# First stage of a four-layer graph network: casting transfers from GpSimd, three bf16 adjacency buffers, x a graph ahead

## What is computed

```python
h = jnp.maximum(_layernorm(x, axis=-1), 0.0)
w = _masked_row_softmax(transpose(adj))    # rows: 1/degree where there is an edge
region = jnp.matmul(w, features)           # features = h
region = jnp.matmul(region, kernel_1) + bias_1
region = _batch_norm(region, gamma_1, beta_1)        # over all graphs and nodes
people = jnp.matmul(jnp.transpose(w, (0, 2, 1)), region)
people = jnp.matmul(people, kernel_2) + bias_2
people = _batch_norm(people, gamma_2, beta_2)
x = x + people
```

## Time and profile before

| | us |
|---|---|
| Median of 3 runs | 1920.06 |
| Lowest, highest | 1919.37, 1922.35 |
| Profiled execution | 1929.35 |
| Its span, first to last instruction | 1927.6 |
| TensorE busy | 1584.4 (82%) |
| VectorE busy | 1387.6 (72%) |
| ScalarE busy | 1212.3 (63%) |
| GpSimd busy | 124.2 (6%) |

### The profile page before, as it was taken

One profiled execution on the slowest core, in us unless ns is written; L12 is line 12 of the kernel. 1 busy time (PEld: TensorE's weight loads), 2 busy tenths in 40 slices (PEclk: granted clock), 3 DMA queues, 4 the chain that ended last, 5 costly groups with the idle time before them and its releaser, 6 DMA issues. The chain is left out here.

```text
span 1927.6 us, 34910 instructions
## 1 busy us (share of the span) xinstructions
PE 1584.4 (82%) x13252; PEld 1288.4 (67%) x13252; DVE 1387.6 (72%) x3809; ACT 1212.3 (63%) x1905; POOL 124.2 (6%) x73
## 2 busy tenths in 40 slices
PE   3878878699646879889898888988889988898873
PEld 3778778455344757768677686776868767686572
DVE  5666665488546668878888788887788877887663
ACT  4777777122136567777777677776677767776552
POOL 0100100000000000000000000000000000010000
PEclk9998989799857989999999999999999999999986
DMA  6777775267331102022030220302203022020111
GB/s 217 283 253 283 263 251 201 86 242 246 140 105 35 54 23 88 17 84 78 23 99 21 79 77 23 98 15 86 77 23 92 17 90 78 23 66 10 46 33 35
DMA packets 106156, 195.64 MB, mean 101 GB/s; under 512 B 9088, under 2 KB 58880, under 8 KB 103936
## 3 DMA queue, kind: packets, MB, share of 16 engines
q1 hardware_dynamic: 103680, 184.98, 29.4%
q10 hardware_dynamic: 2304, 8.39, 1.1%
HBM read 151.40 MB, written 41.94 MB: 100 GB/s over the span
## 5 line engine op out<-in xcount | busy, mean ns | idle before, releaser
L1278 PE MATMUL ps<-fac_A,mask_A 128*128 128x258 f16 x2048 | 236.9, 275 | 36.1 <-DVE prod L910 24.8
L1278 PE MATMUL ps<-fac_C,mask_C 128*128 128x258 f16 x2048 | 237.3, 275 | 18.1 <-DVE mask_C L928 12.7
L1278 PEld LDWEIGHTS ps<-fac_A,mask_A 128*128 128x128 fp8e4 x2048 | 199.0, 98 | 74.2 <-DVE prod L910 31.7
L1345 PE MATMUL ps<-hV,wts 128*128 128x129 f32 x2048 | 243.0, 276 | 3.5 <-DVE prod L910 1.8
L1345 PEld LDWEIGHTS ps<-hV,wts 128*128 128x128 f32 x2048 | 236.7, 193 | 4.7 <-DVE prod L910 2.3
L1278 PEld LDWEIGHTS ps<-fac_C,mask_C 128*128 128x128 fp8e4 x2048 | 198.2, 98 | 53.7 <-issue 7.6
L953 DVE SCALAR_TENSOR_TENSOR wts<-lk,wts 128x1024 f32<-128x1024 f32 x128 | 154.9, 1221 | 90.6 <-ACT wts L1199 90.6
L1198 ACT ACTIVATE lk<-ps 128x1024 f32<-128x1024 f32 x128 | 131.9, 1031 | 111.3 <-PE ps L1336 87.8
L299 ACT ACTIVATE maskT<-ps 128x1024 fp8e4<-128x1024 bf16 x128 | 130.3, 1018 | 75.9 <-PE ps L338 69.6
L1199 ACT ACTIVATE wts<-ps,shiftB 128x1024 f32<-128x1024 f32 x128 | 143.5, 1121 | 0.0
L1177 ACT ACTIVATE mask_C<-s_row,steep_t_C 128x1024 fp8e4<-128x1024 f32 x128 | 141.7, 1141 | 0.0
(11 more groups left out here) (248 smaller groups left out, 3372.0 us busy)
## 6 DMA issues: line engine op xcount, KB each, us to landing
adj_r<-in_adj SPq DMA_DIRECT2D x128, 512.0 KB, 5.8
maskT_scratch<-maskT SPq DMA_DIRECT2D x16, 1024.0 KB, 6.8
ring_A<-maskT_scratch SPq DMA_DIRECT2D x64, 256.0 KB, 3.2
off<-maskT_scratch SPq DMA_DIRECT2D x32, 512.0 KB, 6.5
ring_C<-maskT_scratch SPq DMA_DIRECT2D x64, 256.0 KB, 4.1
xa<-in_x SPq DMA_DIRECT2D x16, 512.0 KB, 4.1
whT_scratch<-whT_s ACTq DMA_DIRECT2D x16, 512.0 KB, 6.4
whT_b<-whT_scratch SPq DMA_DIRECT2D x16, 512.0 KB, 4.8
```

Of the source, the lines that this page charges most:

```text
L1278: last = nc.tensor.matmul(Q_SLOTS[c % 2][:, k, 0:XW], m_fp8[x][:, k, j, c * P:c * P + P], fac[x][:, k, j, :], start=(j == 0), stop=(j == T ...
L1345: last = nc.tensor.matmul(Q_SLOTS[c // 2 % 2][:, c % 2, 0:PW], wts[:, j, c * P:c * P + P], hV[b % 2][:, j, :], start=(j == 0), stop=(j == ...
```

## The change

All of it is in the first stage and the set-up block ahead of it. `g_acc`, the raw row buffers `adj_r` and VectorE's casts are gone.

- GpSimd issues transfers that read int32 rows from HBM and write bf16 into `adj_b`, which now has three graph buffers. `load_adj(pool, b)` issues eight of 512 KB read. Graph 0 is issued in the set-up block, graph 1 ahead of the first power, graph 2 behind it, and graph b + 2 behind the power for graph b. From graph 3 on the issue waits until all products of the graph that used the buffer are done.
- x has two buffers. SP loads the first two in the set-up block and graph b after `a_h` of graph b - 2.
- VectorE normalises (`normed`, eight instructions), then clips while it writes the high part (`high`) and clips and subtracts for the low part (`low`). ScalarE's `normed` is gone. VectorE waits for the power in `shifts` at c = 3.
- The Gram product accumulates in its PSUM bank over all graphs, and the moments block reads the bank.
- whT is kept in two halves of 256 KB, one at c = 7 of the same graph, one at c = 3 of the next. TensorE waits for a kept half at the first and fifth `sums`.
- TensorE begins a graph's transposes when the eight transfers have landed, and waits for `a_h` only ahead of the first product.
- Memsets in the first stage shrink to the columns that need ones.

```diff
-            adj_r = sba("adj_r", [P, NA, N], i32)
-            adj_b = sba("adj_b", [P, 2, T, N], bf16)
-            xa = sba("xa", [P, T, P])
+            adj_b = sba("adj_b", [P, AB, T, N], bf16)
+            xa = sba("xa", [P, 2, T, P])
...
+            def load_adj(pool, b):
+
+                if b >= AB:
+                    pool.wait_ge(a_wh_made, (b - AB + 1) * T)
+                for r in range(T):
+                    pool.dma_start(adj_b[:, b % AB, r, :], adj[b, r * P:r * P + P, :]).then_inc(a_adj_in[b % AB][r], 16)
...
+                @block.gpsimd
+                def _(pool):
+                    pool.memset(ident[:, :], 0.0).then_inc(ident_zero, 1)
...
+                    load_adj(pool, 0)
...
                 @block.sync
                 def _(sp):
...
+                    for b in range(2, B):
+                        sp.wait_ge(a_h, b - 1)
+                        sp.dma_start(xa[:, b % 2, :, :], x_v[b]).then_inc(a_x_in[b % 2], 16)
 
                 @block.gpsimd
                 def _(pool):
-                    for b in range(0, B):
+                    def rstd(b):
                         pool.wait_ge(a_var, b + 1)
                         pool.tensor_tensor(rs_a[:, :], rs_a[:, :], mhalf[:, :], ALU.pow).then_inc(a_rstd, 1)
 
+                    load_adj(pool, 1)
+                    rstd(0)
+                    load_adj(pool, 2)
+                    for b in range(1, B):
+                        rstd(b)
+                        if b + 2 < B:
+                            load_adj(pool, b + 2)
...
+                    def shifts(b):
+                        dve.wait_ge(a_rstd, b + 1)
+                        nc.vector.scalar_tensor_tensor(sf_a[:, :], mv_a[:, :, 0], -1.0, rs_a[:, :], ALU.mult, ALU.mult)
+                        dve.drain()
+
+                    def normed(b, h):
+                        for t in range(h * T // 2, (h + 1) * T // 2):
+                            nc.vector.tensor_scalar(xa[:, b % 2, t, :], xa[:, b % 2, t, :], rs_a[:, t:t + 1], sf_a[:, t:t + 1],
+                                                    ALU.mult, ALU.add)
+
+                    def high(b):
+                        dve.drain()
+                        nc.vector.tensor_scalar(x0[:, b % 2, :, 0:P], xa[:, b % 2, :, :], 0.0, None, ALU.max)
+
+                    def low(b):
+                        dve.drain()
+                        nc.vector.scalar_tensor_tensor(x0[:, b % 2, :, GW:X0W], xa[:, b % 2, :, :], 0.0, x0[:, b % 2, :, 0:P],
+                                                       ALU.max, ALU.subtract).then_inc(a_h, 1)
...
+                    def graph(b):
+                        more = b + 1 < B
                         for c in range(T):
...
+                            tail(b, c)
+                            if more and c < 2:
+                                stats(b + 1, c)
+                            if more and c == 1:
+                                moments(b + 1)
+                            if more and c == 3:
+                                shifts(b + 1)
+                            if more and 3 <= c < 5:
+                                normed(b + 1, c - 3)
+                            if more and c == 5:
+                                high(b + 1)
+                            if more and c == 6:
+                                low(b + 1)
...
+                    def keep_whT(b, h):
+
+                        n = 2 * b + h
+                        act.wait_ge(a_sums_made, n + 1)
+                        if n > 0:
+                            act.wait_ge(a_whT_out, n * 16)
+                        nc.scalar.copy(whT_s[:, :], psWT[:, h * HALF:(h + 1) * HALF]).then_inc(a_whT_kept, 1)
+                        act.wait_ge(a_whT_kept, n + 1)
+                        act.dma_start(whT_dram[b, :, h * HALF:(h + 1) * HALF], whT_s[:, :]).then_inc(a_whT_out, 16)
...
-                        nc.tensor.matmul(psG, whn[:, c, 0:P], whn[:, c, :], start=(c == 0), stop=(c == T - 1))
+                        if b > 0 and c % HT == 0:
+                            pe.wait_ge(a_whT_kept, 2 * b - 1 + c // HT)
+                        nc.tensor.matmul(psG, whn[:, c, 0:P], whn[:, c, :], start=(b == 0 and c == 0), stop=(b == B - 1 and c == T - 1))
...
+                    for b in range(B):
+                        first = b == 0
+                        for r in range(T):
+                            pe.wait_ge(a_adj_in[b % AB][r], (b // AB + 1) * 16)
...
+                            if c == 0:
+                                pe.wait_ge(a_h, b + 1)
...
-                    nc.vector.tensor_scalar(eg[:, :], g_acc[:, :], 1.0 / (B * N), None, ALU.mult).then_inc(m_eg, 1)
+                    nc.vector.tensor_scalar(eg[:, :], psG, 1.0 / (B * N), None, ALU.mult).then_inc(m_eg, 1)
```

More of the change, by code:

```diff
@@ L104, in gnn_stack_kernel @@
                   (be2_sb[:, :], be2.rearrange("(p o) -> p o", o=1))]
[L106 to L137, removed]
         whT_dram = nc.dram_tensor("whT_scratch", (B, P, N), fp32).ap()
@@ L183, in _ @@
                 def _(sp):
-                    def graph(b, first):
-                        if not first:
-                            sp.wait_ge(a_h, b)
-                        sp.dma_start(xa[:, :, :], x_v[b]).then_inc(a_x_in, 16)
-                        for r in range(T):
-                            if not (first and r < NA):
-                                sp.wait_ge(a_adj_used, b * T + r - NA + 1)
-                            sp.dma_start(adj_r[:, r % NA, :], adj[b, r * P:r * P + P, :]).then_inc(a_adj_in[r % NA], 16)
@@ L231, in tail, with stats, moments @@
-                    def tail(b, par, c, first):
+                    def stats(b, h):
+                        if h == 0:
+                            dve.wait_ge(a_x_in[b % 2], (b // 2 + 1) * 16)
+                        for t in range(h * T // 2, (h + 1) * T // 2):
+                            nc.vector.bn_stats(st_a[:, t, :], xa[:, b % 2, t, :])
+                    def moments(b):
+                        dve.drain()
+                        for t in range(T):
+                            nc.vector.bn_aggr(mv_a[:, t, :], st_a[:, t, :])
+                        dve.drain()
+                        nc.vector.tensor_scalar(rs_a[:, :], mv_a[:, :, 1], LN_EPS, None, ALU.add).then_inc(a_var, 1)
@@ L258, in _ @@
[L258 to L268 removed]
+                    stats(0, 0)
@@ L270, in _ @@
+                    stats(0, 1)
+                    moments(0)
+                    shifts(0)
+                    normed(0, 0)
+                    normed(0, 1)
+                    high(0)
+                    low(0)
+                    for b in range(B):
+                        graph(b)
                 @block.scalar
                 def _(act):
-                    def normed(b, t0, t1):
-                        if t0 == 0:
-                            act.wait_ge(a_shift, b + 1)
-                        for t in range(t0, t1):
-                            last = nc.scalar.activation(xa[:, t, :], xa[:, t, :], ACT.Relu, bias=sf_a[:, t:t + 1], scale=rs_a[:, t:t + 1])
-                        if t1 == T:
-                            last.then_inc(a_norm, 1)
```

164 lines of the change are left out of this document (62 added, 102 removed).

## The result

| | us |
|---|---|
| before, median (range) of 4 runs | 1920.9 (1919.37 to 1922.35) |
| after, median (range) of 4 runs | 1863.15 (1859.67 to 1867.42) |
| ratio, 95% interval | 0.9697 (0.9678 to 0.9715) |
| profiled execution, before and after | 1929.35 and 1867.42 (span 1865.6) |

The change saves 57.8 us in the medians and 61.9 between the profiled executions; 72.1 was forecast. The time lies inside the range, 15 us above the forecast of 1848.0. To find where it went I split both traces at these marks: the first and the last product of the stage, the start of the moments, and the first and the last of VectorE's instructions that write `wts` in the long later part (L953 of the kernel before, L947 of the kernel after).

What follows compares the result with a forecast made beforehand. TensorE (14.2 us per graph) and DMA (14.8) were taken to alternate where they could overlap. Savings of 3.3 at the start, 68.0 between products and 0.8 at the end make 72.1: 1929.35 to 1857.3, less 9.3 is 1848.0; range 1827 to 1935.

Steps and rivals of the forecast that it cites:

- The period, 15.3: First stage: us per graph, from floors of 14.2, 14.2 and 14.7 plus 0.6 for `whn` wait and jitter; 19.9 before.
- floor of 14.7: GpSimd's queue in the first stage: issues, power and VectorE's work until `a_h` need P >= 10.7 + 4X per graph.
- X: Cost of one DMA issue from GpSimd, put between 0.5 and 2.0 us and taken as 1.0.
- the geometric middle: Choice of 1.0 us per GpSimd issue, between SP's 0.5 per issue and GpSimd's 2.0 for small arithmetic.
- I take no stall: ScalarE's whT halves: each store lands within four columns, 7.1 us (median 6.4); at 8.8 it would cost 1.7 per half.
- The start, 24.6: Time of the first product in us, in general 8.6 + 16X, against 27.86 before; 3.3 saved.
- the second block begins at 9.9: Start: set-up block's first issues run from 1.5 to 9.5 us, then the next block begins.
- rivals 2 and 3: Adjacency's casting transfers: second, somewhat slower, 1888 us (about 1870 at 341 GB/s), chance 0.13; third, slow, about 2000, chance 0.20.
- The end, -0.8: Last product to moments: whT half 0.5 us faster to copy and perhaps 0.3 to land, against 5.7 before.
- (1): Rival: GpSimd's queue becomes the first stage's bound, X from 1.5 to 2; 1905 us at 1.75; chance 0.14.
- (4): Rival: adjacency buffers come free only when a graph's products are done, so gap and order stay; 1920 us; chance 0.04.
- (5): Rival: VectorE's normed and high, some 3 us per graph, block GpSimd's issues; 1871 us; chance 0.04.

Runs made afterwards that it cites:

- e_start: Changed kernel with weight loads and the turning of kernel_1 moved out of the set-up block, so that it waits for no weights: ratio 0.9653 to the kernel before.
- e_pool_b: Changed kernel with two superfluous powers over 24 columns on GpSimd ahead of each graph's own: 1921.19 us.
- e_start2: As e_start, with graph 0's adjacency also issued in the first stage's own block and the first power ahead of graph 1's issues: ratio 0.9679 to the kernel before.

## Why the prediction was right, point by point

**Direction and mechanism: right.** TensorE's stand before each graph and VectorE's wait for raw rows went, the clock came back to 1.00, and VectorE and ScalarE came out at 9.7 and 11.8 busy, where 9.6 and 11.8 were summed from rows. VectorE's agreement is partly luck: the g_acc add, said to be removed, was not taken off the sum, which would be 9.3.

**The period, 15.3: measured 15.04, but for another reason.** The sum was a floor of 14.7 and 0.6 for the wait for `whn` and jitter. The floor failed: it was GpSimd's chain with X = 1.0. X is 0.54, so this chain's floor is 12.9, GpSimd waits up to 7.0 us per graph for the products and then for VectorE's variance, and the largest floor is TensorE's 14.2. The lower bound, SP's 0.5 per issue of the same tile, was the row to go by; the geometric middle had nothing behind it but the width of the bracket. The addition came out too small: 0.84 stand above 14.2, of which the waits for `whn` are 9.5 / 15 = 0.6. What stretches these waits is the edge that the forecast saw and set to nothing, the half kept at c = 7. "I take no stall" failed: ScalarE waits 1.02 for the store and then copies. The mistake was to set the median landing of 6.4 against four whole columns, 7.1. The store before this half was issued at 112.79, after a copy that had itself waited, and ScalarE came to the next copy at 119.35 - 1.02 = 118.33: 5.5 us later, while the median store takes 6.5. So 0.5 too much in the floor and 0.24 too little above it left the period 0.26 off.

**The start, 24.6: measured 30.0, and the term failed by more than that.** By the formula 8.6 + 16X it would have been 17.2 at the measured X of 0.54. The step that failed is "the second block begins at 9.9": it let the block end with the last issue. Two things keep it: weights that land at 17.5 in the adjacency's wake, and, once these are taken away, GpSimd's own transfers (16.9 in `e_start`). The mechanism was 12.8 us off; by luck the X taken too large hid 7.4 of them, and 5.4 were left. The forecast gave the block's weights no wait at all; in the trace before they landed 2.1 to 2.3 us after their issue, with no adjacency beside them.

**The casting transfers: right.** At the plain pace, 207 GB/s written for 414 read; rivals 2 and 3 fell with it, and TensorE has no wait for `adj_b` with a transfer as releaser. The Trainium skill (DMA: Bandwidth & Descriptors, Measured) has 341 GB/s for 1 MB issued from GpSimd. That is a figure for one transfer; the stream here, eight of 512 KB read one behind the other, moved 414 read, so the price of rival 2 by that figure did not come about.

**The end, -0.8: measured +0.5.** The half store lands in 6.5 us at the median, as long as the whole one before, so nothing was gained there.

**Rivals.** (1) fell: X is far under 1.5. Right in kind, as `e_pool_b` shows with 8.4 us more in the queue. (4) fell with the graph starts. (5) fell: in the steady stage the issues are over before VectorE normalises, and at the start, where both do meet, the issues do not slow down. GpSimd and VectorE in the kernel after:

```profile
25.42 4.42 POOL L151 DMA_DIRECT2D adj_b<-in_adj  x8
25.75 2.13 DVE L234 TENSOR_SCALAR xa<-xa,rs_a,sf_a 128x128 f32<-128x128 f32 x8
27.97 0.70 DVE L239 TENSOR_SCALAR x<-xa 128x1024 f16<-128x1024 f32 x1
```

Eight issues take 4.42 beside `normed` and `high`, and 4.42 at 1.69 with VectorE nearly idle. No lock shows; the sentence of the Trainium skill (SBUF — State Buffer, Who interferes with whom) is not borne out for these issues.

**The sum.** 72.1 up to the moments against 70.4 measured: +5.4 at the start and 1.3 at the end, less 5.0 between the products. Behind it the forecast set nothing, and 10.4 us were lost and 1.7 and 0.3 gained. That "behind this stage only one operand changes" is true of the instructions, not of the clock. The 62 between the profiled executions against 58 between the medians is that the one before stood 8.4 over its median and the one after 4.3.

## What to carry to other kernels

Price an unseen issue by the nearest row of the same operation, and use the middle of a bracket only where no row is nearer than the other. Look for what ends a block before moving transfers into it: small loads behind a saturating stream, and transfers that GpSimd has still under way, cost 12 us here. A saving measured at the end of a stage is to be checked at the end of the kernel: here 70 us became 58 to 64. And take a second trace of the kernel before, when small differences are to be read from it.

## What the runs showed of the hardware

- A casting transfer from int32 to bf16 keeps the pace of a plain one by the bytes read (414 against 408 to 418 GB/s); the profile counts the bytes written.
- GpSimd issues a transfer of 128x1024 in 0.54 us, as fast as SP with 0.5.
- Beside the adjacency's stream the three loads of 0.5 KB that the set-up block waits for landed 11.3 to 12.5 us after their issue (2.1 to 2.2 before), and SP's issues of the loads of `a` took 1.2 to 1.8 us each.
- A block in which GpSimd has issued transfers ended only when these had landed: 6.1 to 16.9 us with nothing else to wait for (`e_start`). With only SP's two loads of x under way it ended at about 2.2, before they had landed (`e_start2`).
- The same later instructions took from 1209.8 to 1227.3 us in 14 traces, in step with TensorE's busy time (1070 to 1087) and with the granted clock.
